# A row maximum over score tiles: seven quarter tiles in place of two half tiles are taken off VectorE

## The reference, cut to what matters

```python
qkv = einsum('btd,de->bte', x, w_qkv) + b_qkv          # x: 4 x 2048 x 256
q, k, v = heads(q), heads(k), heads(v)                 # 16 heads of 16
q, k = rope(q), rope(k)
attn = softmax(einsum('bhqd,bhkd->bhqk', q, k) / 4)    # 2048 x 2048 per head
out = einsum('bhqk,bhkd->bhqd', attn, v)
x = layernorm(x + out @ w_out + b_out)
x = layernorm(x + ffn(x))                              # silu(gate) * up, int weights
```

## Time and profile before

| | before |
|---|---|
| median of 3 runs (lowest to highest) | 2852.1 us (2850.74 to 2855.02) |
| the profiled execution | 2853.19 us |
| its span | 2851.1 us |
| PE busy | 2820.5 us (99%) |
| DVE busy | 2691.3 us (94%) |
| ACT busy | 2578.5 us (90%) |
| POOL busy | 1416.2 us (50%) |
| mean granted clock of PE | 0.989 |

### The profile page before, as it was taken

The page is one execution under the profiler, slowest core; times in us unless marked ns, Lnnn a source line. Parts: engine busy times, 40 slices in busy tenths (PEclk is TensorE's granted clock), DMA queues, the critical chain, the costliest instruction groups (busy, mean ns, idle before and its releaser), DMA issues. The chain is left out here.

```text
span 2851.1 us, 70512 instructions
## 1 busy us (share of the span) xinstructions
PE 2820.5 (99%) x27022; PEld 882.6 (31%) x27022; DVE 2691.3 (94%) x3088; ACT 2578.5 (90%) x4778; POOL 1416.2 (50%) x4133
## 2 busy tenths in 40 slices
PE   8989999999999999999999999999999999999998
PEld 4531222222222222222222222222222222246665
DVE  7989999999999999999999999999999999947777
ACT  5756999999999999999999999999999999975655
POOL 7851444444444444444444444444444444436553
PEclk9978999999999999999999999999999999999999
DMA  5431111111111111111111111111111111233431
GB/s 196 141 119 27 37 35 36 35 36 35 36 35 36 35 36 35 35 35 36 35 36 35 36 36 35 36 35 36 36 36 35 35 36 35 70 93 89 119 97 38
DMA packets 121519, 146.56 MB, mean 51 GB/s; under 512 B 52832, under 2 KB 87520, under 8 KB 121180
## 3 DMA queue, kind: packets, MB, share of 16 engines
q1 hardware_dynamic: 120892, 142.02, 17.3%
q10 hardware_dynamic: 288, 0.01, 0.0%
HBM read 106.30 MB, written 35.13 MB: 50 GB/s over the span
## 5 line engine op out<-in xcount | busy, mean ns | idle before, releaser
L102 DVE TENSOR_REDUCE tile_max<-s_ps 128x1 f32<-128x1024 f32 (+1 forms) x2048 | 2273.9, 1181 | 4.3 <-PE s_ps L91 2.5
L1076 ACT ACTIVATE probs<-bank_ps 128x512 f32<-128x512 f32 x4096 | 2188.9, 603 | 67.0 <-PE bank_ps L956 40.5
L966 PE MATMUL bank_ps<-probs,kept_v 128*17 128x256 f32 x16384 | 1283.2, 385 | 0.0
L91 PE MATMUL s_ps<-k,q 64*128 64x512 f16 x4096 | 1267.0, 387 | 11.1 <-DVE tile_max L102 9.3
L956 PE MATMUL bank_ps<-q,k 64*128 64x512 f16 x4096 | 1252.5, 382 | 1.2 <-ACT probs L1076 0.8
L1211 POOL TENSOR_TENSOR larger<-spared 128x256 f32<-128x256 f32 x1107 | 342.8, 310 | 659.3 <-ACT spared L1051 582.3
L956 PEld LDWEIGHTS bank_ps<-q,k 64*128 64x128 f16 x4096 | 271.9, 93 | 910.7 <-ACT probs L1076 823.7
L966 PEld LDWEIGHTS bank_ps<-probs,kept_v 128*17 128x17 f32 x16384 | 271.8, 95 | 806.4 <-ACT probs L1076 412.1
L1220 POOL TENSOR_TENSOR spared<-spared,larger 128x256 f32<-128x256 f32 x984 | 318.0, 323 | 81.9
L1213 POOL TENSOR_SCALAR larger<-larger 128x256 f32<-128x256 f32 x1107 | 261.4, 236 | 96.8
L91 PEld LDWEIGHTS s_ps<-k,q 64*128 64x128 f16 x4096 | 259.5, 94 | 50.4 <-DVE tile_max L102 46.5
(11 more groups left out here) (119 smaller groups left out, 1625.2 us busy)
## 6 DMA issues: line engine op xcount, KB each, us to landing
q<-q_parts SPq DMA_DIRECT2D x193, 128.0 KB
k<-k_parts SPq DMA_DIRECT2D x193, 128.0 KB
x_t<-in_x_t SPq DMA_DIRECT2D x16, 512.0 KB, 7.6
q_parts<-parts SPq DMA_DIRECT2D x32, 256.0 KB, 2.6
k_parts<-parts SPq DMA_DIRECT2D x32, 256.0 KB, 2.6
heads_out<-sums SPq DMA_DIRECT2D x256, 32.0 KB, 2.0
kept_v<-heads_out SPq DMA_DIRECT2D x16, 512.0 KB, 5.9
kept_v<-inverses_out SPq DMA_DIRECT2D x32, 256.0 KB
```

What stands on the lines that cost most here:

```text
L91: mm = pe.matmul(s["s_ps"][g % 2][:, j * BANK:(j + 1) * BANK], s["q"][h % 2][rows, r // KW * P:(r // KW + 1) * P], s["k"][h % 2][rows, at: ...
L102: dve.tensor_reduce(s["tile_max"][h % 2][:, r // KW, r % KW:r % KW + 1], s["s_ps"][g % 2][:, columns], AX.X, ALU.max).then_inc(s["s_read"], 1)
L966: mm = pe.matmul(o_ps[h][c * 32:c * 32 + VM, at:at + HALF], t["kept"][:, h, kt, :], probs[(h * KT + kt) % RING][:, c * BANK + at:c * BANK ...
L1076: act.activation(probs[(h * KT + kt) % RING][:, c * BANK:(c + 1) * BANK], st_ps[n][:, :], ACT.Exp, scale=scale).then_inc(exp_done, 1)
```

## The change

- Seven tiles of a head are split in place of two: r = 0, 3, 6, 9 (a batch of four) and r = 17, 20, 23 (a batch of three), in each head from the third on; the last head has only the first batch.
- ACT copies columns 0 to 255 of the tile (`keep_quarter`), behind the odd exponential ahead of the place it had for a half tile.
- DVE reduces columns 512 to 1023 first, then waits for that copy and reduces columns 256 to 511 into a fourth column of `tile_max`. `s_read` is signalled by the second reduction, and PE has no wait for the copy any more.
- POOL folds a whole batch at once, in eight levels of three operations (the last with one more), from two buffers in turn; the join takes four columns, in six operations again.
- The transpose stands behind tile `TURN` = 4, not 2.

```diff
-    ROWS = (2, 20)
+    BATCHES = ((0, 3, 6, 9), (17, 20, 23))
...
-    TURN = 2
+    TURN = 4
...
-    SPARED = [h * MAXES + r for h in range(2, HEADS) for r in ROWS][:-1]
-    LEVELS = 9
-    FOLDS = 3 * LEVELS
+    SPARES = [[h * MAXES + r for r in rows] for h in range(2, HEADS) for rows in BATCHES][:-1]
+    SPARED = [g for batch in SPARES for g in batch]
+    LEVELS = 8
+    RUNS = 2
+    FOLDS = 3 * LEVELS + RUNS - 1
...
                     wait(pe, s_read, g - 1)
-                    if g - 2 in SPARED:
-                        pe.wait_ge(half_kept, SPARED.index(g - 2) + 1)
...
-            def keep_half(n):
-
-                act.wait_ge(half_done, n + 1)
-                wait(act, folded, FOLDS * n)
-                act.copy(spared[:, :], s_ps[SPARED[n] % 2][:, 0:BANK]).then_inc(half_kept, 1)
+            def keep_quarter(batch, i):
+
+                g = SPARES[batch][i]
+                act.wait_ge(half_done, SPARED.index(g) + 1)
+                wait(act, folded, FOLDS * (batch - 1))
+                act.copy(spared[batch % 2][:, i, :], s_ps[g % 2][:, 0:QUARTER]).then_inc(quarter_kept, 1)
...
-                    g = (h + 1) * MAXES + LEAD + e // 2
-                    if e % 2 == 0 and g in SPARED:
-                        keep_half(SPARED.index(g))
+                    g = (h + 1) * MAXES + LEAD + (e + 1) // 2
+                    if e % 2 == 1 and g in SPARED:
...
-                own = slice(BANK, WIDE) if g in SPARED else slice(0, WIDE)
-                tile_maximum(dve, s, g, T, own)
+                if g not in SPARED:
+                    tile_maximum(dve, s, g, T, slice(0, WIDE))
+                    return
+                dve.tensor_reduce(tile_max[h % 2][:, r // KW, r % KW:r % KW + 1], s_ps[g % 2][:, BANK:WIDE],
+                                  AX.X, ALU.max).then_inc(bank_read, 1)
+                dve.wait_ge(quarter_kept, SPARED.index(g) + 1)
+                dve.tensor_reduce(tile_max[h % 2][:, r // KW, KW + 1:KW + 2], s_ps[g % 2][:, QUARTER:BANK],
+                                  AX.X, ALU.max).then_inc(s_read, 1)
```

More of the change, by code:

```diff
@@ L782, in attend @@
     TAKE_WHOLE = (22, 23)
-    ROWS = (2, 20)
+    BATCHES = ((0, 3, 6, 9), (17, 20, 23))
+    MOST = max(len(rows) for rows in BATCHES)
+    QUARTER = BANK // 2
     INVERT = 10
-    TURN = 2
+    TURN = 4
     JOINS = 6
@@ L820, in attend @@
         max_scaled = sb("max_scaled", [P, 32])
-        spared = sb("spared", [P, BANK])
-        larger = sb("larger", [P, BANK // 2])
-        more_top = sb("more_top", [P, QT])
+        spared = [sb(f"spared{i}", [P, MOST, QUARTER]) for i in range(2)]
+        larger = sb("larger", [P, MOST, QUARTER // 2])
+        more_top = sb("more_top", [P, QT, KW])
+        pair_top = sb("pair_top", [P, QT, KW])
         max_parts = [sb(f"max_parts{i}", [P, PARTS, 32], F16) for i in range(2)]
@@ L840, in attend @@
         s_done, s_read = s["s_done"], s["s_read"]
+        bank_read = sem("bank_read")
         half_done = sem("half_done")
-        half_kept = sem("half_kept")
+        quarter_kept = sem("quarter_kept")
         folded = sem("folded")
+        lowered = sem("lowered")
         head_max = sem("head_max")
@@ L1079, in _ @@
                         drain(h - 1)
-                    g = (h + 1) * MAXES + LEAD + e // 2
-                    if e % 2 == 0 and g in SPARED:
-                        keep_half(SPARED.index(g))
+                    g = (h + 1) * MAXES + LEAD + (e + 1) // 2
+                    if e % 2 == 1 and g in SPARED:
+                        for batch, tiles in enumerate(SPARES):
+                            if g in tiles:
+                                keep_quarter(batch, tiles.index(g))
                     if h == HEADS - 1 and e % 2 == 1:
@@ L1093, in clear @@
                     dve.memset(head_top[i][:, :], 0.0).then_inc(cleared, 1)
-                    dve.memset(tile_max[i][:, :, KW:KW + 1], LOWEST).then_inc(cleared, 1)
+                    dve.memset(tile_max[i][:, :, KW:KW + 2], LOWEST).then_inc(cleared, 1)
             def maximum(g):
@@ L1182, in cut, with larger_of @@
                                    ALU.subtract).then_inc(max_cut, 1)
+            def larger_of(a, b, more, out, sem, step):
+                pool.tensor_tensor(more, b, a, ALU.subtract).then_inc(sem, 1)
+                pool.wait_ge(sem, step + 1)
+                pool.tensor_scalar(more, more, -LOWEST, 0.0, ALU.min, ALU.max).then_inc(sem, 1)
+                pool.wait_ge(sem, step + 2)
+                pool.tensor_tensor(out, a, more, ALU.add).then_inc(sem, 1)
             def join(h):
@@ L1187, in join @@
                 pool.wait_ge(s_read, (h + 1) * MAXES)
-                wait(pool, folded, FOLDS * sum(g < (h + 1) * MAXES for g in SPARED))
+                wait(pool, bank_read, sum(g < (h + 1) * MAXES for g in SPARED))
+                wait(pool, folded, FOLDS * sum(batch[0] < (h + 1) * MAXES for batch in SPARES))
                 wait(pool, max_turned, h - 1)
[L1190 to L1208, removed]
-                    wait(pool, folded, step)
[L1210 to L1220, removed]
-                    wide //= 2
+                if h == HEADS - 1:
+                    pool.wait_ge(lowered, 1)
@@ new lines, in join, with fold @@
+                step = JOINS * h
+                wait(pool, head_max, step)
+                larger_of(tile_max[i][:, :, 0:KW], tile_max[i][:, :, KW:2 * KW], more_top[:, :, :], pair_top[:, :, :],
+                          head_max, step)
+                pool.wait_ge(head_max, step + 3)
+                larger_of(pair_top[:, :, 0], pair_top[:, :, 1], more_top[:, :, 0], head_top[i][:, 0:QT],
+                          head_max, step + 3)
+            def fold(batch):
+                tiles = SPARES[batch]
+                h, n, wide = tiles[0] // MAXES, len(tiles), QUARTER // 2
+                pool.wait_ge(quarter_kept, SPARED.index(tiles[-1]) + 1)
+                held = spared[batch % 2]
+                for k in range(LEVELS - 1):
+                    step = FOLDS * batch + 3 * k
+                    wait(pool, folded, step)
+                    larger_of(held[:, 0:n, 0:wide], held[:, 0:n, wide:2 * wide], larger[:, 0:n, 0:wide],
+                              held[:, 0:n, 0:wide], folded, step)
+                    wide //= 2
+                step = FOLDS * batch + 3 * (LEVELS - 1)
+                more = larger[:, 0:n, 0:1]
+                pool.wait_ge(folded, step)
+                pool.tensor_tensor(more, held[:, 0:n, 1:2], held[:, 0:n, 0:1], ALU.subtract).then_inc(folded, 1)
+                pool.wait_ge(folded, step + 1)
+                pool.tensor_scalar(more, more, -LOWEST, 0.0, ALU.min, ALU.max).then_inc(folded, 1)
+                pool.wait_ge(folded, step + 2)
+                wait(pool, head_max, JOINS * (h - 1))
+                rows = [g % MAXES // KW for g in tiles]
+                starts = [i for i in range(n) if i == 0 or rows[i] != rows[i - 1] + 1]
+                for at, end in zip(starts, starts[1:] + [n]):
+                    pool.tensor_tensor(tile_max[h % 2][:, rows[at]:rows[end - 1] + 1, KW:KW + 1], held[:, at:end, 0:1],
+                                       larger[:, at:end, 0:1], ALU.add).then_inc(folded, 1)
@@ L1238, in _ @@
                 cut(h)
-                for n in range(len(SPARED)):
-                    if SPARED[n] // MAXES == h + 1:
-                        fold(n)
+                if h == HEADS - 3:
+                    unspared = slice(BATCHES[-1][0] // KW, QT)
+                    pool.wait_ge(head_max, JOINS * (h + 1))
+                    pool.memset(tile_max[(HEADS - 1) % 2][:, unspared, KW:2 * KW], LOWEST).then_inc(lowered, 1)
+                for batch, tiles in enumerate(SPARES):
+                    if tiles[0] // MAXES == h + 1:
+                        fold(batch)
                 if h == HEADS - 2:
@@ L1551, in layer @@
         s["s_ps"] = [ctx.enter_context(nc.psum_tensor(f"s_ps{i}", [P, 2 * BANK], F32)) for i in range(2)]
-        s["tile_max"] = [sb(f"tile_max{i}", [P, T // P, T // (2 * BANK) + 1]) for i in range(2)]
+        s["tile_max"] = [sb(f"tile_max{i}", [P, T // P, T // (2 * BANK) + 2]) for i in range(2)]
         s["s_done"], s["s_read"] = sem("s_done"), sem("s_read")
```

## The result

| | before | after |
|---|---|---|
| median of the runs, us | 2851.97 (2850.74 to 2855.02) | **2891.48** (2888.02 to 2895.48) |
| ratio, 95% interval | | 1.0137 [1.0121, 1.0153] |
| profiled execution, its span | 2853.2, 2851.1 | 2894.47, 2892.7 |
| a head, from transpose to transpose | 35.66 | 36.45 |

A forecast was written before the change was run, and what follows sets the result against it. PE was taken to bound most of a head, DVE only tiles 18 to 21. Quiet heads 35.65 us, 39 disturbed ones 36.85: +46 us on the profiled 2853.2, 2898 against the median; range 2848 to 2916.

The forecast's parts named there:

- 60 x 0.38 won: Each head before any stall: all parts of the edit together take 0.38 us off, from 35.66 to 35.28.
- 21 x 0.37: Quiet heads: from transpose to first transposed scores 4.88 us usable, chain 5.25, so PE stalls 0.37; head 35.65 us.
- 39 x 1.57 lost: Heads 13 to 51, 16 KB instruction packet meeting the chain: PE stalls 1.57 us, head 36.85; 39 heads if the slip halves.
- The half tiles' 0.14 and 0.07: PE's steps at half tiles 2 and 20: 0.14 and 0.07 us a head lost before, forecast to come back.
- worst price of 0.68: Split tile's second piece on DVE: 0.33 us if overlapping like full tiles, 0.68 if neither piece overlaps and its wait is late.
- third rival: DVE: split pieces at 0.68 + 0.41 save 0.04 a tile, DVE needs 36.2 us and binds again; 2918 us, chance 0.09.
- The estimate by the Trainium skill's rule: DVE: 120 cycles per PSUM-source instruction beside its columns; a split tile would cost 1.05 us and save 0.14.
- In time by 2 us: POOL's fold and join of the last batch end 2 us before DVE reaches the new transpose.
- 4.88 against 5.25: Usable us from transpose behind tile 4 to first transposed scores, against the chain of cut, store and row loads until landing.
- 6.45 in the mean of those 26: Mean chain in us of heads 20 to 45 of the kernel before, taken as the disturbed heads' chain.
- The first (quiet only, 2850): Rival: other fetches move too or packets use other DMA engines; every head takes 35.65 us, 2850 in all; chance 0.10.
- the second (the chain doesn't bind, 2829): Rival: DVE runs closer behind PE or lands sooner; 60 x 0.38 = 23 us come off, 2829 us; chance 0.10.

## Why the prediction was right

**The sum.** Forecast for the 60 heads: 60 x 0.38 won, and 21 x 0.37 and 39 x 1.57 lost, together +46. Measured: 0.44 won a head, 26.4; PE's first step with a head's `scores_t` 2.22 where a free one is 1.09, 67.7 lost; some 4 more in the steps behind four of the waits, at the lower clock (below). Together +45, and 3 come off ahead of the heads and behind them. The forecast was 6.5 us too high, of which these 3 were the ramp and tail that it left out.

**What the edit saves.** 0.44 a head, not 0.38. The half tiles' 0.14 and 0.07 came back whole, and no step on PE at tiles 18 to 21 takes 1.13 any more. The step in which a new head's tile 0 is made lost 0.12 before and 0.06 now, where I had expected no difference: that is the rest. The split tile was priced right in the sum: its pieces start 0.60 and 0.34 ahead of their successors (654.39, 654.99, 655.33), and nothing on DVE is idle between them (0.0 in both groups). A full tile's step being 1.13, it saves 0.19. (For the second piece alone the prediction has a worst price of 0.68 in one place and 0.41 in its third rival; it lasts 0.42 and costs 0.34.) The estimate by the Trainium skill's rule was 0.14 ("VectorE: DVE Perf Modes", errata section). These rows don't bear it out as a spacing: from start to start 256 columns take 0.34, 512 take 0.60 and 1024 take 1.13. The last 512 of these cost 0.53, so the first 512 leave 0.07 us beside the columns, and with so little a split costs less than the rule has it. As durations the rule's figures, an estimate of 1.19, 0.66 and 0.39, are near the measured 1.21, 0.68 and 0.42. The copy takes 367 ns where I had ~0.37 and hinders no even matmul: each stands 0.23 us behind its odd one, in all steps but the one with the copy of the sums and the first with a head's `scores_t`.

**POOL.** In time by 2 us was the forecast, 2.32 it is. "At TURN = 2 nothing would be left" was nearly right: 0.24 us were left. But the join is in time with that, and the run at TURN = 2 is the best.

**The room and the chain.** 4.88 against 5.25 gave 0.37 in a quiet head; measured are a chain of 5.34 in the mean of the twelve quiet ones and a quiet head of 35.57 where 35.65 was forecast, 0.35 above the 35.22 without a wait.

**The disturbed heads.** 37 for 39 (39 with the two at the edges), heads 18 to 54 for 13 to 51, and the slip 0.10 for 0.09: right. The term that was off is "6.45 in the mean of those 26", carried over to them: their chain is 6.17. What makes it less is not shown. The 26 weren't all disturbed either: heads 21 and 34 of the kernel before have 5.26 and 5.40, and in the kernel after heads 39, 40 and 42, with a packet 2.4 to 2.6 behind the transpose, have 5.24 to 5.27. And I had counted one kind of packet; 11 more heads have an 8 KB one and 6.01. The two errors are 37 x 0.28 = 10 us one way and 11 x 0.7 = 8 the other (with heads 17 and 55 in the first row, 10 and 6). That they nearly cancel is luck.

The rule on 256 instructions in a 16 KB line (the Trainium skill, "Advanced Engine Details and Errata", ISA Cache) gave estimates of 0.09 a head for 770 instructions and 0.19 for 772. The trace agrees at both in the mean: 0.10 in the kernel after, 0.18 with the two waits put back. It is what made the number of disturbed heads come out. The packet doesn't move evenly, though: in the quiet heads up to 16 it stays at 6.2 to 7.0 behind the transpose, is at 4.4 in head 18, at 2.5 in head 32 and at 1.5 in head 48.

**Rivals.** The first (quiet only, 2850) falls with the table of heads, the second (the chain doesn't bind, 2829) with all 60 heads waiting, the third (split tiles eat the saving) with the run at TURN = 3, where the split tiles are the same and the kernel is faster. The second describes what the change would have been at TURN = 2.

## What to carry to other kernels

In a loop whose engines are all nearly full, moving the head of a latency chain (here one transpose of 0.2 us) to a later place cost little here until the room fell below the chain, and then its whole displacement in every turn; read the room and the chain from the trace before you move it, and put it as early as its input is ready, even if only by 0.2 us. Take the chain's disturbed length, not the shortest, as what has to fit. And try the schedule number of an edit apart from its work: here the work won 27 us and the number lost 67.

## What was not expected of the hardware

**Two instructions more made it faster.** A 16 KB packet that loads instructions lengthens a small DMA on the critical path when they fall together (that the two meet on one of the 16 DMA engines is likely, not shown), and the period of the packets against the loop decides how many turns are hit: 37 heads with 770 instructions on PE, 18 with 772, 0 with the same 770 and another start, for 36.45, 36.09 and 35.87 us a head. In the heads that they hit, the 16 KB ones add in the mean 0.4 to 1.1 us to a chain of 5.3 to 5.4 (least with TURN = 3 and LEAD = 11, most in the kernel before). That the 8 KB ones do the same rests on the heads in which they lie between 1.7 and 3.2 us behind the transpose; no run moved them.

**A wait of PE in the stream can cost its clock too.** Head 17, PE's timeline:

```profile
840.17 0.39 PE L961 MATMUL bank_ps<-q,k 64*128 64x512 f16 x1
...
842.90 0.58 PE L961 MATMUL bank_ps<-q,k 64*128 64x512 f16 x1 [2.34 <-issue]
...
844.43 0.60 PE L961 MATMUL bank_ps<-q,k 64*128 64x512 f16 x1
...
846.21 0.39 PE L961 MATMUL bank_ps<-q,k 64*128 64x512 f16 x1
```

And the windows view ahead of it, behind it and after that:

```profile
838.00:840.00 2.00, 2.00 (x28) 0.56 (x24) 2.00 (x3) 2.00 (x6) 0.00 (x0) 1.00 0.00 1
842.90:845.90 3.00, 3.00 (x22) 0.54 (x22) 1.59 (x2) 1.43 (x3) 2.70 (x4) 0.50 0.49 108
846.00:848.00 2.00, 2.00 (x28) 0.49 (x24) 1.87 (x2) 1.52 (x4) 1.66 (x5) 1.00 0.14 57
```

PE had stood for 2.34 us; behind that the granted clock is 0.50, the level of 1.2 GHz, and the same matmul takes 0.58 in place of 0.39. It is back at 1.00 by 846. This cost 0.7 to 1.3 us in the steps behind the wait, in heads 17, 29, 45 and 47 of the kernel after. Beside head 17 they aren't the longest waits: heads 18 and 43 waited for 1.86 and 1.83 and lost nothing, heads 29, 45 and 47 for 1.63 to 1.76. At TURN = 5, where the heads wait for 1.3 to 3.8 us, 18 of them lose 0.8 to 2.1 us this way, and others nothing behind waits of up to 2.3. So the wait of "over 2.3 us" in what was expected of that run is no limit: shorter ones cost the clock too. A long stall on PE can thus cost somewhat more than its length, and the price is not a steady one.
